# A decoder layer on one core: how the stacked query and key parts of cross-attention get into SBUF

## The reference, cut to what matters

```python
x = x + _L0_xattn_ref(_layernorm(x, axis=-1), ctx_2048, ctx_2048, L0_xattn_gamma)

def _L0_xattn_ref(q, k, v, gamma):       # q, k, v: 16 x 256 x 512, N_HEAD = 8
    qh = q.reshape(B, h, dq, Lq)         # dq = 256 // 8 = 32: a head is 32 rows (tokens)
    kh = k.reshape(B, h, dq, Lk)
    vh = v.reshape(B, h, dv, Lk)
    qk = jnp.einsum('bhdq,bhdl->bhql', qh, kh) * scale
    sm = jax.nn.softmax(qk, axis=-1)
    ret = jnp.einsum('bhql,bhdl->bhdq', sm, vh)
    return gamma * ret.reshape(B, Dv, Lq)
```

## Time and profile before

| | us |
|---|---|
| median of three runs | 2818.88 (2817.76 to 2822.01) |
| the profiled execution, its own time | 2815.54 |
| its span, first to last instruction | 2813.8 |
| cross-attention in it, first DMA of the stage to the last exponentials | about 2017 to 2611 |

### The profile page before, as it was taken

One profiled execution on the slowest core, in us unless ns is written; L12 is line 12 of the kernel. 1 busy time (PEld: TensorE's weight loads), 2 busy tenths in 40 slices (PEclk: granted clock), 3 DMA queues, 4 the chain that ended last, 5 costly groups with the idle time before them and its releaser, 6 DMA issues. The chain is left out here.

```text
span 2813.8 us, 38435 instructions
## 1 busy us (share of the span) xinstructions
PE 2639.5 (94%) x13448; PEld 1978.8 (70%) x13448; DVE 1737.7 (62%) x3567; ACT 990.8 (35%) x2474; POOL 862.5 (31%) x698
## 2 busy tenths in 40 slices
PE   3699999999999999999999999999599999999795
PEld 2488888888888888888888888888444444444573
DVE  7466656666555565556665666666467777675557
ACT  2222222322222232222223222222257777776220
POOL 2111111322111142111123211211258887777100
PEclk9999999999999999999999999999889999999797
DMA  8512111332111232112222213210367777762003
GB/s 312 188 56 95 61 60 61 108 107 86 61 60 60 102 124 75 60 61 81 99 75 90 75 61 105 76 60 31 124 182 188 185 187 185 190 188 62 20 1 120
DMA packets 165098, 290.08 MB, mean 103 GB/s; under 512 B 11568, under 2 KB 78128, under 8 KB 162864
## 3 DMA queue, kind: packets, MB, share of 16 engines
q1 hardware_dynamic: 164912, 287.65, 32.7%
HBM read 194.81 MB, written 92.27 MB: 102 GB/s over the span
## 5 line engine op out<-in xcount | busy, mean ns | idle before, releaser
L439 PE MATMUL pj<-xnt,whi 128*128 128x512 f32 x2048 | 704.2, 405 | 16.2 <-DMA xnt<-xt_scratch 16.2
L519 ACT ACTIVATE pr<-sc,nmx 128x128 f32<-128x128 f32 (+1 forms) x512 | 211.1, 417 | 934.7 <-DVE nmx L591 934.7
L394 POOL TENSOR_TENSOR qt<-rot,swp 128x512 f32<-128x512 f32 x128 | 166.1, 1298 | 1127.4 <-DVE swp L572 1127.4
L439 PEld LDWEIGHTS pj<-xnt,whi 128*128 128x128 f32 x2048 | 385.6, 188 | 108.5 <-DMA xnt<-xt_scratch 16.6
L990 DVE TENSOR_REDUCE xnmx<-xsc 128x1 f32<-128x512 f32 x512 | 336.7, 685 | 162.6 <-PE xsc L810 159.6
L439 PE MATMUL pj<-xnt,wlo 128*128 128x512 f32 x1024 | 398.7, 389 | 0.0
L780 POOL TENSOR_TENSOR xprt<-xprt 128x512 f32<-128x512 f32 x256 | 320.3, 1280 | 116.2 <-PE xob L830 87.5
L436 PE MATMUL pj<-whi,xnt 128*128 128x512 f32 x1024 | 351.7, 405 | 0.0
L932 ACT ACTIVATE xprt<-xst 128x512 f32<-128x512 f32 x512 | 290.6, 595 | 112.1 <-PE xst L819 108.8
L570 DVE TENSOR_TENSOR rot<-pj,trig 128x512 f32<-128x512 f32 x256 | 177.0, 691 | 226.8 <-PE pj L439 226.8
L591 DVE TENSOR_REDUCE nmx<-sc 128x1 f32<-128x128 f32 (+1 forms) x512 | 158.6, 352 | 177.3 <-PE sc L465 172.8
(11 more groups left out here) (185 smaller groups left out, 4344.1 us busy)
## 6 DMA issues: line engine op xcount, KB each, us to landing
xnt<-xt_scratch SPq DMA_DIRECT2D x64, 1024.0 KB, 8.0
x_scratch<-xio SPq DMA_DIRECT2D x64, 512.0 KB, 3.5
xio<-x_scratch SPq DMA_DIRECT2D x48, 512.0 KB, 4.1
qst<-sq_scratch SPq DMA_DIRECT2D x96, 256.0 KB, 5.1
kst<-sk_scratch SPq DMA_DIRECT2D x96, 256.0 KB, 5.7
xt_scratch<-parts SPq DMA_DIRECT2D x16, 1024.0 KB, 4.7
sq_scratch<-qp SPq DMA_DIRECT2D x32, 512.0 KB, 8.0
sk_scratch<-kp SPq DMA_DIRECT2D x32, 512.0 KB, 4.8
```

Of the source, the lines that this page charges most:

```text
L394: nc.gpsimd.tensor_tensor(qk["QK".index(kind)][h][:, :, :].rearrange("p b n -> p (b n)"), rot[r % 2][:, :], swp[r % 2][:, :], ALU.add).the ...
L439: last = nc.tensor.matmul(bank[:, :], wpart[:, w, i * HD:(i + 1) * HD], moving, start=(k == 0), stop=(k == 3 * CB - 1))
L519: nc.scalar.activation(pr[:, a % 4, lo:hi], SC[a % 2][:, lo:hi], ACT.Exp, bias=nmx[:, a % 4, t:t + 1], accum_out=rsum[:, a % 4, t:t + 1]). ...
```

## The change

The scratch tensors and the DMA writes go. `qp` and `kp` become two buffers each, used in turn. A new `spread(m)` on SP waits for both rests, then as before for the last transposed score of tile m - 3, and issues 24 copies from SBUF to SBUF, 3 combinations by 2 stacks by 4 heads, each of 32 partitions by 2 KB (64 KB). It stands where read_stacks stood. All 24 count on `s_st`, for which PE waits as before. `q_round(m)` and `k_round(m)` now wait until the copies of tile m - 2 have landed.

```diff
--- before.py
+++ after.py
@@ -623,7 +623,7 @@
             dve.wait_ge(s_bn, 2 * TILES)
 
 
-def cross_attention(nc, x1, ctx_in, gamma, sq, sk, mv2, mv3, x2, cst):
+def cross_attention(nc, x1, ctx_in, gamma, mv2, mv3, x2, cst):
 
 
     ident = cst["ident"]
@@ -641,6 +641,7 @@
         PARTS = 3
         KS = PARTS * XD
         KM = KS + 2
+        COPIES = 16 * PARTS * XPT
         AHEAD = 6
         RING = 5
         STACKS = 3
@@ -651,8 +652,8 @@
         shift = sb("shift2", [P, TILES], F32)
         cin = sb("cin", [P, 4, D], F32)
         xn = sb("xn2", [P, D], F32)
-        qp = sb("qp", [P, 2, D], F32R)
-        kp = sb("kp", [P, 2, D], F32R)
+        qp = [sb(f"qp{i}", [P, 2, D], F32R) for i in range(2)]
+        kp = [sb(f"kp{i}", [P, 2, D], F32R) for i in range(2)]
         qst = [sb(f"qst{i}", [P, XPT, D], F32R) for i in range(STACKS)]
         kst = [sb(f"kst{i}", [P, XPT, D], F32R) for i in range(STACKS)]
         vt = sb("vt", [P, 2, CB, P], F32)
@@ -680,7 +681,6 @@
         s_ci = [sem(f"x_ci{i}") for i in range(4)]
         s_qn, s_qhi, s_qlo = sem("x_qn"), sem("x_qhi"), sem("x_qlo")
         s_khi, s_klo = sem("x_khi"), sem("x_klo")
-        s_qw, s_kw = sem("x_qw"), sem("x_kw")
         s_st = [sem(f"x_st{i}") for i in range(STACKS)]
         s_row = [sem(f"x_row{i}") for i in range(STACKS)]
         s_ones = sem("x_ones")
@@ -715,25 +715,18 @@
                     sp.wait_ge(s_klo, m - 3)
                 sp.dma_start(cin[:, m % 4, :], cv[m]).then_inc(s_ci[m % 4], 16)
 
-            def write_queries(m):
+            def spread(m):
                 sp.wait_ge(s_qlo, m + 1)
-                sp.dma_start(sq[m % 2].rearrange("h p d -> p h d"), qp[:, :, :].bitcast(F32)).then_inc(s_qw, 16)
-
-            def write_keys(m):
                 sp.wait_ge(s_klo, m + 1)
-                sp.dma_start(sk[m % 2].rearrange("h p d -> p h d"), kp[:, :, :].bitcast(F32)).then_inc(s_kw, 16)
-
-            def read_stacks(m):
-                sp.wait_ge(s_qw, 16 * m + 16)
-                sp.wait_ge(s_kw, 16 * m + 16)
                 if m >= STACKS:
                     sp.wait_ge(s_ts, 16 * (m - STACKS) + 16)
-                qv = sq[m % 2].rearrange("h (j r) d -> h r j d", j=XPT)
-                kv = sk[m % 2].rearrange("h (j r) d -> h r j d", j=XPT)
                 for c in range(PARTS):
                     rows = slice(XD * c, XD * (c + 1))
-                    sp.dma_start(qst[m % STACKS][rows, :, :].bitcast(F32), qv[c // 2]).then_inc(s_st[m % STACKS], 16)
-                    sp.dma_start(kst[m % STACKS][rows, :, :].bitcast(F32), kv[c % 2]).then_inc(s_st[m % STACKS], 16)
+                    for stack, parts, part in ((qst, qp, c // 2), (kst, kp, c % 2)):
+                        for j in range(XPT):
+                            src = parts[m % 2][XD * j:XD * (j + 1), part, :]
+                            sp.dma_start(stack[m % STACKS][rows, j, :].bitcast(F32),
+                                         src.bitcast(F32)).then_inc(s_st[m % STACKS], 16)
 
             def max_rows(m):
                 for k, (part, here) in enumerate(((mhi, s_mhi), (mlo, s_mlo))):
@@ -747,10 +740,7 @@
             load_x(4)
             for n in range(-3, TILES):
                 if tile(n + 2):
-                    read_stacks(n + 2)
-                if tile(n + 3):
-                    write_queries(n + 3)
-                    write_keys(n + 3)
+                    spread(n + 2)
                 if n >= 0 and tile(n + 4):
                     load_context(n + 4)
                 if n >= 0 and tile(n + 5):
@@ -763,12 +753,12 @@
         def _(pool):
             def q_rest(m):
                 pool.wait_ge(s_qhi, m + 1)
-                nc.gpsimd.tensor_tensor(qp[:, 1, :], xn[:, :], qp[:, 0, :].bitcast(F32),
+                nc.gpsimd.tensor_tensor(qp[m % 2][:, 1, :], xn[:, :], qp[m % 2][:, 0, :].bitcast(F32),
                                         ALU.subtract).then_inc(s_qlo, 1)
 
             def k_rest(m):
                 pool.wait_ge(s_khi, m + 1)
-                nc.gpsimd.tensor_tensor(kp[:, 1, :], cin[:, m % 4, :], kp[:, 0, :].bitcast(F32),
+                nc.gpsimd.tensor_tensor(kp[m % 2][:, 1, :], cin[:, m % 4, :], kp[m % 2][:, 0, :].bitcast(F32),
                                         ALU.subtract).then_inc(s_klo, 1)
 
             def pair_sum(n, k):
@@ -804,7 +794,7 @@
             def scores(g, q):
                 m, h = g // CB, g % CB
                 if h == 0 and q == 0:
-                    pe.wait_ge(s_st[m % STACKS], 16 * 2 * PARTS * (m // STACKS + 1))
+                    pe.wait_ge(s_st[m % STACKS], 2 * COPIES * (m // STACKS + 1))
                 if 4 * g + q >= 2:
                     pe.wait_ge(s_mx, 4 * g + q - 1)
                 nc.tensor.matmul(SC[q % 2][:, :], qst[m % STACKS][0:KS, h, q * P:(q + 1) * P],
@@ -912,13 +902,15 @@
 
             def q_round(m):
                 act.wait_ge(s_qn, m + 1)
-                act.wait_ge(s_qw, 16 * m)
-                nc.scalar.activation(qp[:, 0, :], xn[:, :], ACT.Copy).then_inc(s_qhi, 1)
+                if m >= 2:
+                    act.wait_ge(s_st[(m - 2) % STACKS], 2 * COPIES * ((m - 2) // STACKS + 1))
+                nc.scalar.activation(qp[m % 2][:, 0, :], xn[:, :], ACT.Copy).then_inc(s_qhi, 1)
 
             def k_round(m):
                 act.wait_ge(s_ci[m % 4], 16 * (m // 4 + 1))
-                act.wait_ge(s_kw, 16 * m)
-                nc.scalar.activation(kp[:, 0, :], cin[:, m % 4, :], ACT.Copy).then_inc(s_khi, 1)
+                if m >= 2:
+                    act.wait_ge(s_st[(m - 2) % STACKS], 2 * COPIES * ((m - 2) // STACKS + 1))
+                nc.scalar.activation(kp[m % 2][:, 0, :], cin[:, m % 4, :], ACT.Copy).then_inc(s_khi, 1)
 
             def exps(s, h):
                 act.wait_ge(s_ts, 4 * s + h + 1)
@@ -1430,8 +1422,6 @@
 def decoder_layer(nc, x, ctx_in, w_all, gamma, router_w, router_b, expert_w, expert_b, rope, out):
     xt = nc.dram_tensor("xt_scratch", [B, P, 2, CB, L], F32).ap()
     x1 = nc.dram_tensor("x1_scratch", [B, P, TB, D], F32).ap()
-    sq = nc.dram_tensor("sq_scratch", [2, 2, P, D], F32).ap()
-    sk = nc.dram_tensor("sk_scratch", [2, 2, P, D], F32).ap()
     ctx = ExitStack()
     with ctx:
         def sb(name, shape, dt):
@@ -1455,7 +1445,7 @@
             layer_norm_1(nc, x, w_all, xt, cst, wts)
             self_attention(nc, x, w_all, rope, xt, x1, mv2, cst, wts)
         x2 = sb("x2", [P, TILES, D], F32)
-        cross_attention(nc, x1, ctx_in, gamma, sq, sk, mv2, mv3, x2, cst)
+        cross_attention(nc, x1, ctx_in, gamma, mv2, mv3, x2, cst)
         expert_mix(nc, router_w, router_b, expert_w, expert_b, mv3, x2, out, cst)
```

## The result

The changed kernel takes 3112.3 us in the median of 4 runs (3105.6 to 3116.9), beside 2818.6 for the kernel before (4 runs). The ratio is 1.104, with a 95% interval of 1.1015 to 1.106: 294 us slower, where 150 were forecast and the range ended at 231. The profiled execution has a span of 3115.1 us.

A forecast was written before the change was run, and what follows sets the result against it. The prediction took PE to set the time in the steady part; 108 us of stall, rounding and start plus 42 us of clock made 150 us, added to 2818.9 for 2969 us, range 2885 to 3050.

The forecast's parts named there:

- The release, the first use and the place of the cost: From tile m - 3's last transposed score to tile m's first score, 9.43 us to fill a stack; PE would wait there.
- Part 1: Stack fill on SP's queue: 24 issues 0.475 us apart, the last at 10.9 us, stalling PE 3.57 us per tile.
- an argument about partitions: The 0.514 us copy within SBUF gathers 16 partitions into one, while the change's copies go from 32 to 32.
- the rival of dear issues: Copies on SP's queue issue at 0.56 us, restart at 15.1, 5.8 us per tile with the rounding: 3043 us; chance 0.11.
- The landing: A 64 KB copy into the stacks lands 2.0 us after its issue, with ends of 1.8 and 5.1.
- Part 2: ACT's query rounding waits for the same copies as PE, making the first exponential late by 0.1 us per tile.
- Parts 3 and 4: SP's queue, busy 13.8 us of a tile, and DMA traffic, 1.5 MB of reads becoming copies: both change nothing.
- Part 5: Start of cross-attention: PE's first score 0.85 us earlier, then 2.4 us lost at tile 2.
- Part 6: PE's clock falls after the stall in four tiles of five, 1.8 us each: 42 us, ends 0 and 52.
- The rival in which the clock stays: The stall comes in each tile but PE keeps its full clock: 108 us, 2927 us; chance 0.20.
- the two falls that it had seen: Two places in the earlier trace, near 2016 and 2605 us, where PE's clock fell after 3.0 us idle.
- The faster rival: Transfer decides, not issue: at 0.32 us or less per issue PE's wait for the stacks goes, about 2810 us; chance 0.04.

The follow-up runs named there:

- Experiment 5: Kernel before with eight bursts of eight DMAs added behind cross-attention; an issue took 0.59 to 0.60 us within SBUF, 0.42 with scratch memory at one end and 32 rows.
- experiment 6: Changed kernel with six idle matmuls, whose result nobody reads, ahead of PE's wait for the stacks from the fourth tile on: 3075.2 us.
- experiment 2: Changed kernel with only 12 of the 24 copies issued from the fourth tile on, the rest left out: 2824.1 us.
- experiment 11: Changed kernel with four stacks instead of three and four buffers of exponentials instead of five: 3042.0 us.
- experiments 1 and 4: First: changed kernel with 18 of the 24 copies from the fourth tile on, 3001.6 us. Second: kernel before with its six reads cut into 24, 2998.8 us.
- experiment 10: Changed kernel with 8 of the 24 copies issued from ACT's queue, two each in four of ACT's steps: 2961.0 us.

## Why the prediction was wrong

**The release, the first use and the place of the cost: right.** PE's wait at the score line, ended by a DMA, once in every tile, is what the trace shows, and the last copy lands just ahead of the restart.

**Part 1, the price of an issue: this is the term that failed.** The prediction took 0.475 us, from six reads of scratch memory, with ends at 0.37 and 0.56. Measured is 0.634 (0.59 and 0.04 between two). Of the last issue's delay, 15.26 instead of 10.9, the spacing makes 22 x 0.159 = 3.5, the first issue 0.2, and a long issue in this tile 0.7 (0.4 in the mean). Against the 106.4 us that stalls and rounding were to cost in 29 tiles stand 29 x 7.6 = 220, 114 more.

The right price stood in the trace of the kernel before. Maxima move in two copies, one right behind the other, and the prediction called the first of them, at 0.514, the one row within SBUF. The second has a row of its own:

```profile
L742 SPq DMA_DIRECT2D qst<-xmlo x32: 537/589/1199, 2055.6 to 2583.7; - x32
```

0.589 and 0.045 between two are the 0.634 that were measured. The prediction set the row of 0.514 aside with an argument about partitions. Experiment 5 shows that the argument had it the wrong way round: partitions and size make no difference within SBUF, and at 32 rows the ends do. Even the rival of dear issues, at 0.56, was too cheap: it took the copy that goes out by itself after a wait, and not the one behind it.

The landing, 2.0 us, was right to the digit of the page.

**Part 2, ACT's wait: right.** The wait is 7.8 us long and covered by PE's. Behind it the rounding ends at 2434.45, 0.08 after PE's first transposed score has started, and in the tiles of experiment 6 in which the clock held, first use to release took 7.3 us with the same wait of the rounding, as in experiment 2, where the rounding hardly waits. So the 0.1 us was nothing.

**Parts 3 and 4, SP's queue and the traffic: right in kind.** SP's wait for the release is still there, 73.2 us in 26 tiles, so the queue itself never set the pace. Its work in a tile is 15.2 + 2.4 = 17.6 and not 13.8 us, though, more than the 17.15 of the old tile. So even without any wait for a release the change could not quite have kept the old time. In experiment 11 this work and the wait for PE's maxima, in turn, are the round that sets the tile.

**Part 5, the start: wrong by the same term.** PE's first score is 3.0 us later, not 0.85 earlier,

```profile
2046.17 1.19 PE L800 MATMUL xsc<-kst,qst 96*128 96x512 f32 x2 [30.25 <-DMA kst<-kp]
```

and tiles 1 and 2 wait too. Without the 3.6 us of the stage ahead, the first two maxima come 5.6 and then 7.0 later, 12.6 us where 1.5 were forecast.

**Part 6, the clock: right in kind, too low in size.** The clock falls in every tile, and a fall costs more than 1.8 us: 2.2 over the tiles of before, 65 us in 29 tiles and not 42. The prediction took the way back as 3.9 us; in the tile above it was 5.4, and 5.4 x (1 - 0.23/0.42) is 2.4. The rival in which the clock stays has fallen, also at shorter stalls than the one forecast: experiments 1 and 4 stall for 3.9 us in the mean, experiment 10 for 2.5, and slow scores follow in every tile. The prediction weighed its stall against the 3.0 us of the two falls that it had seen, and that was no bound: in the tile shown of experiment 10 the clock fell 1.3 us after the last matmul.

The Trainium skill, page "TensorE: Matmul & The Clock Gate", section "HAM oscillation — how this bites in real kernels", has the engine throttled anew at each wait for a DMA. The traces agree, with the 0.50 in front of the restart above, and with slow transposed scores behind all 29.

**The sum.** 150 forecast, and 114 for the stalls, 23 for the clock and 11 for the start: 298. The spacing of the maxima gives 302 with the 3.6 us of the stage before, the medians 294. With 0.634 for the price and a fall in every tile the same working gives about 3098 us, an estimate (29 x 7.4 for stall and rounding, 52 for the clock, 12 for the start), 14 short of the result.

**The faster rival** lived on issues at 0.32 or less, and there are none: the least of all 768 copies took 0.507.

The Trainium skill, page "DMA: Bandwidth & Descriptors", section "Issuing engines are not separate DMA queues", calls the sequencer's time to initiate a DMA "usually small relative to the DMA itself". For these copies it is not: 0.59 us of issue against an estimated 0.25 of bytes (64 KB at the 265 GB/s of the prediction), and at 24 in a row it sets the tile.

## What to carry to other kernels

Count the issues between a buffer's release and its first use, and price each by a row that has the same two ends and stands, like them, behind another issue; a row of another kind is not the price. Replacing few large transfers by many small ones on one queue saves traffic, and costs one issue for each, so it pays only where the queue has the time, or where the work can be given to a second queue or started ahead of the release. If a buffer is filled barely in time, one more buffer is the first thing to try: it was worth 16 us here, where the shorter way cost 294.

## What the runs showed of the hardware that was not expected

- An issue's price goes by the ends and the rows, not by size: 0.59 to 0.61 us within SBUF at 32, 64, 96 and 128 partitions and from 8 to 192 KB, 0.59 from scratch memory to scratch memory at 32 rows, 0.42 to 0.43 between SBUF and scratch memory at 32 rows and, read into SBUF, at 128, but 0.60 at 64, and 0.51 at 128 written from SBUF. Why is open.
- Single issues in the bursts of 24 took up to 1.95 us, which made 0.4 us a tile in the mean. Their cause was not looked for.
- SP's and ACT's queues issue at the same time and hardly slow each other (0.600 and 0.614 us, beside 0.591 and 0.612 alone).
- The length of a stall alone does not say whether the clock falls. It fell in all 29 tiles with stalls of 3.1 to 5.0 us (experiments 1 and 4), and also with 0.7 to 3.4 us, mean 2.5 (experiment 10). With 2.0 to 3.4 us behind filling matmuls (experiment 6) it fell in 14 of 29: behind one stall of 2.1 us, and not behind one of 3.2. What else decides was not looked for.
